# The twist of a coupling network on half-swapped copies made by transfers, and one gelu issued per batch

## The chip, the cores and the metric

The kernel runs on one core of a Trainium2 chip. The metric is the device time of one launch in microseconds (us). The engines are named as the profile names them: PE (TensorE, with PEld for its weight loads), ACT (ScalarE), DVE (VectorE), POOL (GpSimd) and SP (SyncE, which here issues the DMA transfers).

## The reference

The input x has the shape (4, 1024, 128): four batches b, 1024 tokens, 128 channels. Two blocks follow each other. The first is a layer norm, an attention of 16 heads and a gate from a spiking feed-forward net. The second is a layer norm, a causal attention with position slopes, and a gate from the coupling network below; its output is x + attention * silu(network). The change lies in the coupling network alone:

```python
def _coupling_net(h, w1, b1, w2, b2, w3, b3, w4, b4):
    h = _gelu(h @ w1 + b1)          # 128 -> 128
    h = _gelu(h @ w2 + b2)          # 128 -> 64
    h = _gelu(h @ w3 + b3)          # 64 -> 32
    return jax.nn.sigmoid(h @ w4 + b4)
def _twist(x):
    o_r, o_i, p_r, p_i = jnp.split(x, 4, axis=-1)
    return jnp.concatenate([p_r, -p_i, -o_r, o_i], axis=-1)
for _ in range(NUM_CYCLES):         # 3
    tf = _coupling_net(out, ...)
    combined = 0.7 * gf + 0.3 * tf  # gf: one number per batch
    coupling = BASE_COUPLING + adaptive_range * (combined - 0.5) * 2.0
    out = out + coupling * _twist(out)
```

The twist takes channel c from channel c + 64 (or c - 64), with a sign for each quarter of the channels.

## The kernel before

**Stages.** The launch runs through a prologue, `first_attention`, `middle`, and `second_attention`, with a small `row_maxima` between them. `middle` computes the coupling network for all four batches. Each stage ends in a barrier of all engines, so the next one starts when the slowest engine of `middle` is done.

**Layout in `middle`.** The state is transposed: 128 channels on the 128 partitions, 1024 tokens per batch in the free dimension (`state(b)`, a slice of the tile `y`). `half(b, hf)` is a slice of 512 tokens. The four batches form two streams z of two batches k each, so batch = 2z + k. Three cycles of two streams make six rounds n = 0 to 5, with stream z = n % 2 and cycle n // 2. Round n works on the same state as round n - 2.

**One round.** `first_layer(n, k)` multiplies both halves of a batch by w1 (L1592) and gelu follows on ACT as g1b0 or g1b1 (L1404, 128x1024). `second_layer(n, k)` multiplies by w2, its 64 output channels for one token half in partitions 0 to 63 and for the other half in 64 to 127 (L1599). One gelu, `g2`, then covers both batches (L1404, 128x1024). `third_layer(n)` (L1607) writes batch 0 to partitions 0 to 63 and batch 1 to 64 to 127 of one bank, by two column positions of the array; a gelu `g3` follows (L1404, 128x512). `last_layer(n)` (L1620) spreads the single output over all 128 partitions, so the tanh `t0`, `t1` of `couple(n, k)` (L1425, 128x1024) has the same value on each partition. `twist(n, k)` on DVE then updates the state: two operations on 64 partitions each (L1524) compute (t + offset) * state with the source half read crosswise, and a third on 128 partitions (L1527) adds slope times that to the state; slope carries the signs.

**Order.** It is written out by hand on each engine, and each engine keeps its own order. On PE one pass of the loop is `first_layer(n, 0)`, `last_layer(n - 1)`, `first_layer(n, 1)`, `second_layer(n, 0)`, `second_layer(n, 1)`, `third_layer(n)`. On ACT it is `g3` of round n - 1, `g1b0` of n, `t0` and `t1` of n - 1, `g1b1` of n, `g2` of n. On DVE it is `twist(n - 2, 1)`, `twist(n - 1, 0)`. `first_layer(n, k)` waits for `twist(n - 2, k)`. Around this lies side work for the last quarter of the tokens of the next attention: q, k and v rows and norms, with `low`, `high`, `values`, `norm_peak`. It stands in rounds 0, 1 and 5. After the loop DVE has still `low(0, 1)`, `low(1, 1)`, `twist(4, 1)`, `values(1)`, `norm_peak(1)`, `twist(5, 0)`, four small operations on the flag, and `twist(5, 1)`, its last work in the stage.

**Transfers.** SP issues, at the start of `middle`, six loads of `k_st` and `q_st` (L1370, L1372), then two `load_pair` calls of nine transfers each (L224, L227), then the stores of `q_hl` and `k_hl` for hf = 0 and, late, for hf = 1 (L1382). A semaphore `saved` is raised by POOL (L1395) once it has copied the half of the last batch's state that arrives last.

Of the kernel before, what the change touches and what calls it, by code (L numbers as in the profile page):

```python
# [16 lines left out]
F32 = mybir.dt.float32  # L17
# [3 lines left out]
ALU = mybir.AluOpType  # L21
# [3 lines left out]
P = 128  # L25
B, T, C = 4, 1024, 128
# [192 lines left out]
def load_pair(sp, s, layer, b, gp, sem):  # L219

    tok, own, groups = bass.ds(T * b, T), slice(C // 2 * gp, C // 2 * gp + C // 2), slice(2 * gp, 2 * gp + 2)
    for rows, st, order in ((s["q_hl"][layer], s["q_st"], (0, 0, 1)), (s["k_hl"][layer], s["k_st"], (0, 1, 0))):
        for way, hl in enumerate(order):
            sp.dma_start(st[way::WAYS, groups, :].bitcast(F32),  # L224
                         rows[own, hl:hl + 1, tok].rearrange("(g c) o t -> c g (o t)", g=2)).then_inc(sem, 16)
    for e in range(3):
        sp.dma_start(s["q_st"][WAYS * e + EXTRA::STACK, groups, :].bitcast(F32),  # L227
                     s["q_ext"][layer][H * e + H // 2 * gp:H * e + H // 2 * gp + H // 2, tok].rearrange("(g j) t -> j g t", g=2)).then_inc(sem, 16)
# [1049 lines left out]
STREAMS = 2  # L1278
TINY = 1.0e-12
LAYERS = ("w1b0", "w1b1", "w2b0", "w2b1", "w3", "w4")  # L1280
SQUASHES = ("g1b0", "g1b1", "g2", "g3", "t0", "t1")
SIDE_PS = ("mix31", "xt30", "q30", "k30", "xt31", "v30", "n30", "q31", "k31", "v31", "n31")
SIDE_ACT = ("xt30", "q30", "k30", "xt31", "q31", "k31")
SIDE_DVE = ("mix31", "q30", "k30", "v30", "n30", "q31", "k31", "v31", "n31")
# [2 lines left out]
def middle(nc, a, s):  # L1287
# [5 lines left out]
    with ExitStack() as ctx:  # L1293
        def sb(name, shape, dt=F32):
            return ctx.enter_context(nc.sbuf_tensor(f"n_{name}", shape, dt))

        sem = Semaphores(nc, ctx, "n_")

        ROUNDS = STREAMS * CYCLES
        OWN = B - 1  # L1300
        Q = P // 4
        w1, w2, w3, w4, b1, b2, b3, g1, g2, g3, gb1, gb2, scalars = (s["cn"][name] for name in (
            "w1", "w2", "w3", "w4", "b1", "b2", "b3", "g1", "g2", "g3", "gb1", "gb2", "scalars"))
# [8 lines left out]
        gf, offset = sb("gf", [P, B]), sb("offset", [P, B])  # L1312
        h1 = [sb(f"h1_{k}", [C, 2, HALF]) for k in range(2)]
        h2 = sb("h2", [2 * H1, 2, HALF])
        h3 = sb("h3", [4 * H2, HALF])
        th = [[sb(f"th{z}{k}", [P, 2, HALF]) for k in range(2)] for z in range(STREAMS)]
        change = [s["early"][0][:, k, :, :].bitcast(F32) for k in range(2)]
        late = s["early"][1][:, 0, :, :].bitcast(F32)
        mix, xt31 = late[:, 0, :].rearrange("p (t c) -> p t c", c=C), late[:, 1, :]
        square = [s["ext"][0][:, HALF * hf:HALF * hf + HALF].bitcast(BF16).rearrange("p (z t) -> p z t", z=2) for hf in range(2)]  # L1320
# [3 lines left out]
        ps = [ctx.enter_context(nc.psum_tensor(f"n_ps{z}", [P, 4, HALF], F32)) for z in range(STREAMS)]  # L1324
        pa, pb = ps
        layered, squashed, twisted = (sem.many(x, STREAMS) for x in ("layered", "squashed", "twisted"))
# [2 lines left out]
        chain, twist_link, norm1, peaks = sem("chain"), sem("twist_link"), sem("norm1"), sem("peaks")  # L1329
        xs1_rdy, saved, sq_rdy, peak_turned = (sem(x) for x in ("xs1_rdy", "saved", "sq_rdy", "peak_turned"))  # L1330
        ext_in = sem("ext_in")
        stored = [s[f"stored1{hf}"] for hf in range(2)]
        xt = s["y"][:, :, :].rearrange("p t c -> p (t c)")

        def state(b):
            return xt[:, T * b:T * b + T]
# [4 lines left out]
        def tiles(hf):  # L1341
            return slice(BT * OWN + HT * hf, BT * OWN + HT * hf + HT)

        def by_tile(bank):
            return bank.rearrange("p (t c) -> p t c", c=C)

        def layer_count(n, name):
            return len(LAYERS) * (n // 2) + LAYERS.index(name) + 1

        def squash_count(n, name):  # L1350
            return len(SQUASHES) * (n // 2) + SQUASHES.index(name) + 1

        def batch_count(n, k):
            return 2 * (n // 2) + k + 1
# [7 lines left out]
        def dve_count(name):  # L1362
            return SIDE_DVE.index(name) + 1

        with nc.Block() as block:
            @block.sync
            def _(sp):
                for e in range(3, 6):
                    own = slice(WAYS * e + EXTRA, P, STACK)
                    sp.dma_start(s["k_st"][own, :, :].bitcast(F32),  # L1370
                                 s["k_ext"][H * (e - 3):H * (e - 2), :].rearrange("(g j) t -> j g t", g=NG)).then_inc(ext_in, 16)
                    sp.dma_start(s["q_st"][own, :, :].bitcast(F32), s["one_ext"].rearrange("(g j) t -> j g t", g=NG)).then_inc(ext_in, 16)  # L1372
                for hf in range(2):
                    sp.wait_ge(stored[hf], 32 * (B - 1))
                for gp in range(2):
                    load_pair(sp, s, 1, 0, gp, s["staged"][1][gp])
                for hf in range(2):
                    for z in range(2):
                        sp.wait_ge(side_dve, dve_count(f"{'qk'[z]}3{hf}"))
                        rows = (s["q_hl"][1], s["k_hl"][1])[z]  # L1380
                        tok = slice(T * OWN + HALF * hf, T * OWN + HALF * hf + HALF)
                        sp.dma_start(rows[:, :, tok], parts[hf][:, z, :, :].bitcast(F32)).then_inc(stored[hf], 16)  # L1382
                sp.wait_ge(ext_in, 16 * 6)
# [17 lines left out]
            def _(act):  # L1401
                def gelu(n, name, out, source, bias):
                    z = n % 2
                    nc.scalar.activation(out, source, ACT.Gelu, bias=bias[:, 0:1]).then_inc(squashed[z], 1)  # L1404
# [3 lines left out]
                    gelu(n, f"g1b{k}", h1[k][:, :, :], ps[n % 2][:, 2 * k:2 * k + 2, :], b1)  # L1408

                def second_layer(n):  # L1410
                    act.wait_ge(layered[n % 2], layer_count(n, "w2b1"))
                    gelu(n, "g2", h2[:, :, :], ps[n % 2][:, 0:2, :], b2)

                def third_layer(n):
                    act.wait_ge(layered[n % 2], layer_count(n, "w3"))
# [42 lines left out]
                high(0, 0, pb[:, 2, :])  # L1458
                global_layer(0, 1, pb[:, 1, :])
                second_layer(0)  # L1460
                high(1, 0, pb[:, 3, :])
                for n in range(1, ROUNDS):
# [24 lines left out]
            def _(dve):  # L1487
                ch, links, norm = Chain(dve, chain), Chain(dve, twist_link), Chain(dve, norm1)
# [24 lines left out]
                def twist(n, k):  # L1513
                    z = n % 2
                    out, t = state(2 * z + k), th[z][k][:, :, :].rearrange("p h t -> p (h t)")
                    moved = change[k].rearrange("p h t -> p (h t)")
                    if n < 2 and k == 0:
                        dve.wait_ge(offs, z + 1)
                    dve.wait_ge(squashed[z], squash_count(n, f"t{k}"))
                    if n == 1 and k == 1:  # L1520
                        dve.wait_ge(saved, 1)
                    low_half, high_half = slice(0, P // 2), slice(P // 2, P)
                    for dst, src in ((low_half, high_half), (high_half, low_half)):
                        ins = nc.vector.scalar_tensor_tensor(moved[dst, :], t[src, :], offset[src, 2 * z + k:2 * z + k + 1],  # L1524
                                                             out[src, :], ALU.add, ALU.mult)
                    links.after(ins)
                    nc.vector.scalar_tensor_tensor(out, moved, slope[:, 0:1], out, ALU.mult, ALU.add).then_inc(twisted[z], 1)  # L1527

                means(0)
# [18 lines left out]
                ins = nc.vector.tensor_tensor(mix[:, :, :], by_tile(pb[:, 1, :]), s["xn"][:, tiles(1), :], ALU.add)  # L1548
# [14 lines left out]
                ch.wait()  # L1563
                means(1)
                twist(0, 0)
                for n in range(2, ROUNDS):
                    twist(n - 2, 1)
                    twist(n - 1, 0)
# [17 lines left out]
            def _(pe):  # L1586
# [15 lines left out]

                def third_layer(n):
                    z = n % 2
                    pe.wait_ge(squashed[z], squash_count(n, "g2"))
                    for k in range(2):
                        ins = nc.tensor.matmul(ps[z][2 * H2 * k:2 * H2 * k + 2 * H2, 2, :], w3[:, :], h2[:, k, :],  # L1607
                                               start=True, stop=True, tile_position=(0, 2 * H2 * k))
                    ins.then_inc(layered[z], 1)
# [50 lines left out]
                for t in range(HT):  # L1660
                    for gp in range(2):
                        ins = nc.tensor.matmul(pb[:, 1, t * C:(t + 1) * C], on[2 * gp + 1][:, t * P:(t + 1) * P],
                                               s["wo_x"][:, gp, :], start=gp == 0, stop=gp == 1)
# [9 lines left out]
                second_layer(0, 1)  # L1673
                rows_of(1, 0, half(OWN, 0), pb[:, 3, :])
                third_layer(0)
                global_layer(0, 2, pb[:, 1, :])
                turn_in(1)
# [451 lines left out]
```

## Time and profile before

| | us |
|---|---|
| median of 3 runs | 935.69 (935.6 to 936.01) |
| profiled execution, its own time | 938.43 |
| profiled execution, span of the trace | 936.7 |
| `middle` in the trace, first to last instruction | 545.3 to 627.0 |
| PE busy over the span | 809.0 (86%) |
| ACT busy over the span | 834.5 (89%) |
| DVE busy over the span | 409.8 (44%) |

Starts in the trace are counted from the start of the span. A row of the timeline gives the start, the time taken, the engine, the line and the operation, how many instructions were merged into it, and in brackets how long the engine had idled before it and what released it. PEclk is the mean granted clock of TensorE as a share of full speed.

### The profile page before, as it was taken

The numbers are of one execution on the slowest core, as the hardware profiler recorded it, in microseconds if no ns is written. First come the engines' busy times: TensorE is split into PE (matmuls) and PEld (weight loads), VectorE is DVE, ScalarE is ACT, GpSimd is POOL, SyncE is SP. The second block draws the span as 40 slices with busy tenths as digits, with TensorE's granted clock in tenths as the row PEclk, the third lists the DMA queues.
The fourth block names the chain that finished last, engine by engine and source line by source line (L and its number), as shares of the span: only waits on it lengthen the run. The fifth ranks groups of instructions, "written<-read, shape, count | busy, mean of one in ns | idle before, by whom it ended". The sixth has DMA issues, their size and how long they took to land. (4 is left out here: it accounts for less than half of the span.)

```text
span 936.7 us, 23514 instructions
## 1 busy us (share of the span) xinstructions
PE 809.0 (86%) x9998; PEld 328.0 (35%) x9998; DVE 409.8 (44%) x878; ACT 834.5 (89%) x951; POOL 187.9 (20%) x229
## 2 busy tenths in 40 slices
PE   3859999899999999999999988837888878878876
PEld 2412434234343443433334332213333334333323
DVE  7630264443756437473464867770112111121222
ACT  7659999999999999999999945638999999999995
POOL 2201120130202302022120210001214223233133
PEclk9869999999999999999999999978999999999999
DMA  6972020200201202003001151010202202112000
GB/s 177 291 251 41 2 73 2 71 5 2 96 24 43 77 2 96 25 17 103 3 1 47 47 160 46 0 46 1 73 1 85 70 15 84 29 58 85 13 1 24
DMA packets 32049, 53.53 MB, mean 57 GB/s; under 512 B 5576, under 2 KB 16456, under 8 KB 31944
## 3 DMA queue, kind: packets, MB, share of 16 engines
q1 hardware_dynamic: 31944, 52.02, 17.4%
q8 instruction: 80, 1.31, 0.6%
q14 instruction: 25, 0.20, 0.1%
HBM read 31.29 MB, written 20.71 MB: 56 GB/s over the span
## 5 line engine op out<-in xcount | busy, mean ns | idle before, releaser
L983 ACT ACTIVATE a_probs<-a_sc 128x1024 f32<-128x1024 f32 x512 | 474.5, 1031 | 11.3 <-PE a_sc L1182 10.6
L1858 ACT ACTIVATE a_probs<-a_sc 128x1024 f32<-128x1024 f32 (+1 forms) x320 | 273.5, 957 | 31.1 <-PE a_sc L2010 20.2
L1197 PE MATMUL a_o<-a_probs,vt 128*18 128x256 f32 (+1 forms) x3072 | 273.0, 459 | 0.0
L2045 PE MATMUL a_o<-a_probs,vt 128*18 128x256 f32 (+3 forms) x1920 | 153.4, 428 | 0.6 <-POOL a_probs L1884 0.6
L1182 PE MATMUL a_sc<-q_st,k_st 32*128 32x512 f32 x1024 | 131.7, 502 | 23.3 <-ACT a_probs L983 17.7
L2004 PE MATMUL a_sc<-q_st,k_st 32*128 32x512 f32 (+3 forms) x768 | 80.6, 427 | 62.0 <-ACT a_probs L1858 50.5
L1197 PEld LDWEIGHTS a_o<-a_probs,vt 128*18 128x18 f32 x3072 | 65.4, 97 | 144.3 <-issue 104.4
L1884 POOL TENSOR_SCALAR_AFFINE_SELECT a_probs<-a_probs 128x512 f32<-128x512 f32 x96 | 59.7, 646 | 219.3 <-ACT a_probs L1858 219.3
L1182 PEld LDWEIGHTS a_sc<-q_st,k_st 32*128 32x128 f32 x1024 | 50.7, 184 | 138.2 <-ACT a_probs L983 129.1
L2004 PEld LDWEIGHTS a_sc<-q_st,k_st 32*128 32x128 f32 x768 | 37.9, 184 | 127.3 <-ACT a_probs L1858 112.1
L1010 POOL TENSOR_TENSOR early<-early 128x512 f32<-128x512 f32 x32 | 38.4, 1200 | 185.3 <-DVE early L1120 185.3
L1917 DVE STREAM_TRANSPOSE a_turn<-a_o 128x512 f32<-128x512 f32 x15 | 10.8, 717 | 133.1 <-PE a_o L2045 133.1
L2045 PEld LDWEIGHTS a_o<-a_probs,vt 128*18 128x18 f32 x1920 | 41.8, 97 | 69.1 <-issue 45.5
L1120 DVE TENSOR_SCALAR early<-a_side 128x512 f32<-128x512 f32 x32 | 22.0, 687 | 69.0 <-PE a_side L123 69.0
L1124 DVE TENSOR_SCALAR y<-a_side,rho 128x128 f32<-128x128 f32 x32 | 9.0, 344 | 88.2 <-PE a_side L123 88.2
L1404 ACT ACTIVATE n_h<-n_ps,cn_b 128x1024 f32<-128x1024 f32 (+1 forms) x24 | 24.1, 1006 | 22.0 <-PE n_ps L1592 11.8
L996 POOL TENSOR_TENSOR early<-early,y 128x512 f32<-128x512 f32 x7 | 10.6, 1513 | 144.3 <-DVE early L1135 144.3
L1524 DVE SCALAR_TENSOR_TENSOR early<-n_th,n_offset,y 64x1024 f32<-64x1024 f32 x24 | 30.8, 1285 | 10.3 <-ACT n_th L1425 9.9
L123 PE MATMUL a_side<-proj_t,early 128*32 128x128 f32 x1024 | 33.8, 273 | 0.0
L123 PE MATMUL a_side<-y,fc_t 128*32 128x512 f32 x256 | 33.3, 592 | 0.0
L123 PEld LDWEIGHTS a_side<-proj_t,early 128*32 128x32 f32 x1024 | 29.3, 110 | 5.9
L1018 POOL TENSOR_TENSOR a_square<-parts 128x512 bf16<-128x512 f32 x12 | 15.1, 1257 | 80.4 <-DVE parts L1152 80.4
(242 smaller groups left out, 775.9 us busy)
## 6 DMA issues: line engine op xcount, KB each, us to landing
q_st<-q_hl SPq DMA_DIRECT2D x48, 256.0 KB
k_st<-k_hl SPq DMA_DIRECT2D x48, 256.0 KB
q_hl<-parts SPq DMA_DIRECT2D x12, 512.0 KB, 4.3
k_hl<-parts SPq DMA_DIRECT2D x12, 512.0 KB, 4.7
q_hl<-early SPq DMA_DIRECT2D x4, 512.0 KB, 4.8
k_hl<-early SPq DMA_DIRECT2D x4, 512.0 KB, 5.6
out_dram<-x SPq DMA_DIRECT2D x7, 256.0 KB, 3.9
x<-in_L_attn_x_dram SPq DMA_DIRECT2D x3, 512.0 KB, 5.6
```

The costliest lines, as they stand in the source:

```text
L123: ins = nc.tensor.matmul(out[c:c + COLUMN, :], weight[:, c:c + COLUMN], rows, start=start, stop=stop, tile_position=(0, c))
L983: nc.scalar.activation(probs[t % RING][:, 2 * pair:2 * pair + 2, :], scores[unit % SLOTS][:, :, :], ACT.Exp).then_inc(expd, 1)
L1010: pool.tensor_tensor(hidden[f], hidden[f], hidden[f], ALU.mult).then_inc(hid_rdy, 1)
L1120: ins = nc.vector.tensor_scalar_max(hidden[hf[1]], side[:, :], 0.0)
L1182: ins = nc.tensor.matmul(scores[(2 * t + i // 2) % SLOTS][:, i % 2, :], k_st[part, g, kt * P:(kt + 1) * P], q_st[part, g, qh * HALF:(qh + ...
L1197: ins = nc.tensor.matmul(o_ps[32 * h:32 * h + 2 * W9, c0:c1], vt[b % 2][:, kt, gp, h, W9 * gs:W9 * gs + 2 * W9], probs[t % RING][:, h, c0: ...
L1404: nc.scalar.activation(out, source, ACT.Gelu, bias=bias[:, 0:1]).then_inc(squashed[z], 1)
L1524: ins = nc.vector.scalar_tensor_tensor(moved[dst, :], t[src, :], offset[src, 2 * z + k:2 * z + k + 1], out[src, :], ALU.add, ALU.mult)
L1858: nc.scalar.activation(probs[t % RING][:, 2 * pair:2 * pair + 2, 0:width(t)], scores[unit % SLOTS][:, :, 0:width(t)], ACT.Exp).then_inc(ex ...
L1884: ins = pool.affine_select(out=part, in_=part, compare_op=ALU.is_ge, fill=0.0, base=0, pattern=[[0, G], [1, P]], channel_multiplier=-1)
L2004: ins = nc.tensor.matmul(banks[i][:, at:at + w], k_st[part, g, kt * P:(kt + 1) * P], q_st[part, g, qh * HALF + q0:qh * HALF + q0 + w], sta ...
L2045: ins = nc.tensor.matmul(o_ps[32 * h:32 * h + 2 * W9, q0:q0 + w], vt[b % 2][:, kt, gp, h, W9 * gs:W9 * gs + 2 * W9], probs[t % RING][:, h, ...
```

## The change

`twist` reads a copy of the state with its two partition halves swapped, which two transfers per batch and cycle make: `shift(b)` copies rows 64 to 127 of `state(b)` to rows 0 to 63 of `turned[b]`, and the reverse. With it the two crosswise operations become one on 128 partitions, in place on the copy. The copies of batches 0 to 2 are issued first of all in `middle`, that of batch 3 after `saved`, and those of the later cycles by `shift_again(n)`, after `twist(n, k)`. The gelu of the second layer is issued once per batch (`g2b0`, `g2b1`, each 128x512), and `third_layer` waits for each.

```diff
-SQUASHES = ("g1b0", "g1b1", "g2", "g3", "t0", "t1")
+SQUASHES = ("g1b0", "g1b1", "g2b0", "g2b1", "g3", "t0", "t1")
...
-        change = [s["early"][0][:, k, :, :].bitcast(F32) for k in range(2)]
+        turned = [s["early"][0][:, k, :, :].bitcast(F32).rearrange("p h t -> p (h t)") for k in range(2)]
+        turned += [s["early"][1][:, 1, :, :].bitcast(F32).rearrange("p h t -> p (h t)"), s["ext"][1][:, :]]
...
+        shifted = sem.many("shifted", B)
...
             @block.sync
             def _(sp):
+                def shift(b):
+                    for rows, source in ((slice(0, P // 2), slice(P // 2, P)), (slice(P // 2, P), slice(0, P // 2))):
+                        sp.dma_start(turned[b][rows, :], state(b)[source, :]).then_inc(shifted[b], 16)
+
+                def shift_again(n):
+                    for k in range(2):
+                        sp.wait_ge(twisted[n % 2], batch_count(n, k))
+                        shift(2 * (n % 2) + k)
+
+                for b in range(OWN):
+                    shift(b)
...
+                sp.wait_ge(saved, 1)
+                shift(OWN)
                 for hf in range(2):
+                    if hf == 1:
+                        for n in range(ROUNDS - STREAMS):
+                            shift_again(n)
...
                 def second_layer(n):
-                    act.wait_ge(layered[n % 2], layer_count(n, "w2b1"))
-                    gelu(n, "g2", h2[:, :, :], ps[n % 2][:, 0:2, :], b2)
+                    for k in range(2):
+                        act.wait_ge(layered[n % 2], layer_count(n, f"w2b{k}"))
+                        gelu(n, f"g2b{k}", h2[:, k, :], ps[n % 2][:, k, :], b2)
...
-                    moved = change[k].rearrange("p h t -> p (h t)")
+                    moved = turned[2 * z + k]
...
-                    low_half, high_half = slice(0, P // 2), slice(P // 2, P)
-                    for dst, src in ((low_half, high_half), (high_half, low_half)):
-                        ins = nc.vector.scalar_tensor_tensor(moved[dst, :], t[src, :], offset[src, 2 * z + k:2 * z + k + 1],
-                                                             out[src, :], ALU.add, ALU.mult)
-                    links.after(ins)
+                    dve.wait_ge(shifted[2 * z + k], 32 * (n // 2 + 1))
+                    links.after(nc.vector.scalar_tensor_tensor(moved, t, offset[:, 2 * z + k:2 * z + k + 1], moved, ALU.add, ALU.mult))
                     nc.vector.scalar_tensor_tensor(out, moved, slope[:, 0:1], out, ALU.mult, ALU.add).then_inc(twisted[z], 1)
...
                 def third_layer(n):
                     z = n % 2
-                    pe.wait_ge(squashed[z], squash_count(n, "g2"))
                     for k in range(2):
+                        pe.wait_ge(squashed[z], squash_count(n, f"g2b{k}"))
                         ins = nc.tensor.matmul(ps[z][2 * H2 * k:2 * H2 * k + 2 * H2, 2, :], w3[:, :], h2[:, k, :],
                                                start=True, stop=True, tile_position=(0, 2 * H2 * k))
                     ins.then_inc(layered[z], 1)
```

## Rows read from the trace of the kernel before

**Rows 1.** Groups by line and shape, 540 to 640 us: busy us, mean ns, idle before.

```profile
L1524 DVE SCALAR_TENSOR_TENSOR early<-n_th,n_offset,y 64x1024 f32<-64x1024 f32 x24 | 30.8, 1285 | 10.3 <-ACT n_th L1425 9.9
...
L1404 ACT ACTIVATE n_h<-n_ps,cn_b 128x1024 f32<-128x1024 f32 x18 | 20.0, 1114 | 17.3 <-PE n_ps L1592 11.8 <-PE n_ps L1599 5.5
L1527 DVE SCALAR_TENSOR_TENSOR y<-early,n_slope,y 128x1024 f32<-128x1024 f32 x12 | 15.4, 1284 | 0.4
...
L1404 ACT ACTIVATE n_h<-n_ps,cn_b 128x512 f32<-128x512 f32 x6 | 4.1, 683 | 4.7 <-PE n_ps L1607 4.7
```

**Rows 2.** Timeline of one pass of the loop, up to the gelu of round 4.

```profile
591.82 1.08 PE L1607 MATMUL n_ps<-n_h,cn_w 128*64 128x512 f32 x4 [1.21 <-ACT n_h L1404]
592.83 1.98 PE L1592 MATMUL n_ps<-y,cn_w 128*128 128x512 f32 x4
...
594.04 1.28 DVE L1527 SCALAR_TENSOR_TENSOR y<-early,n_slope,y 128x1024 f32<-128x1024 f32 x1
...
594.85 1.11 ACT L1404 ACTIVATE n_h<-n_ps,cn_b 128x1024 f32<-128x1024 f32 x1 [1.22 <-PE n_ps L1592]
...
595.81 1.98 PE L1592 MATMUL n_ps<-y,cn_w 128*128 128x512 f32 x4
595.95 2.12 ACT L1425 ACTIVATE n_th<-n_ps,n_half_b 128x1024 f32<-128x1024 f32 x2
...
597.96 1.11 ACT L1404 ACTIVATE n_h<-n_ps,cn_b 128x1024 f32<-128x1024 f32 x1
...
599.13 1.08 PE L1599 MATMUL n_ps<-n_h,cn_w 128*64 128x512 f32 x4 [0.32 <-ACT n_h L1404]
...
600.25 1.11 ACT L1404 ACTIVATE n_h<-n_ps,cn_b 128x1024 f32<-128x1024 f32 x1 [1.18 <-PE n_ps L1599]
```

**Rows 3.** Timeline of two narrow windows within `third_layer(4)`.

```profile
601.42 0.65 PE L1607 MATMUL n_ps<-n_h,cn_w 128*64 128x512 f32 x2 [1.22 <-ACT n_h L1404]
...
601.90 0.60 PE L1607 MATMUL n_ps<-n_h,cn_w 128*64 128x512 f32 x2
```

**Rows 4.** Timeline of the end of `middle` and the first matmul after it.

```profile
612.29 0.75 DVE L1492 SCALAR_TENSOR_TENSOR parts<-n_ps,b_col,parts 128x512 fp32r<-128x512 f32 x1 [1.03 <-ACT parts L1436]
...
613.07 2.67 DVE L1524 SCALAR_TENSOR_TENSOR early<-n_th,n_offset,y 64x1024 f32<-64x1024 f32 x2
...
614.99 2.12 ACT L1425 ACTIVATE n_th<-n_ps,n_half_b 128x1024 f32<-128x1024 f32 x2 [1.49 <-PE n_ps L1620]
...
618.48 2.58 DVE L1524 SCALAR_TENSOR_TENSOR early<-n_th,n_offset,y 64x1024 f32<-64x1024 f32 x2
...
623.09 2.58 DVE L1524 SCALAR_TENSOR_TENSOR early<-n_th,n_offset,y 64x1024 f32<-64x1024 f32 x2
625.70 1.28 DVE L1527 SCALAR_TENSOR_TENSOR y<-early,n_slope,y 128x1024 f32<-128x1024 f32 x1
...
629.88 0.80 PE L2004 MATMUL a_sc<-q_st,k_st 32*128 32x512 f32 x4 [11.12 <-DVE a_o L1961]
```

**Rows 5.** Waits by engine and line, 545 to 627 us: us in total, times, longest.

```profile
ACT n_h L1404 <- PE n_ps L1599: 5.5, 6, 1.2
```

**Rows 6.** Timeline of SP, POOL, PE and DVE at the start of `middle`.

```profile
545.28 0.57 SPq L1370 DMA_DIRECT2D k_st<-k_ext  x1
...
560.10 0.61 SPq L1382 DMA_DIRECT2D q_hl<-parts  x1
560.26 0.61 POOL L1395 COPY early<-y 128x512 f32<-128x512 f32 x1 [1.12 <-ACT y L1430]
...
571.93 3.68 PE L1592 MATMUL n_ps<-y,cn_w 128*128 128x512 f32 x4
...
581.90 2.58 DVE L1524 SCALAR_TENSOR_TENSOR early<-n_th,n_offset,y 64x1024 f32<-64x1024 f32 x2
```

**Rows 7.** Windows: busy us of PE, PEld, DVE, ACT, POOL; PEclk, DMA share, GB/s.

```profile
557.00:561.00 4.00, 3.84 (x21) 1.66 (x21) 3.12 (x8) 2.61 (x6) 1.90 (x3) 1.00 0.92 300
...
573.00:577.00 4.00, 4.00 (x13) 1.12 (x12) 0.36 (x1) 1.36 (x2) 0.00 (x0) 0.69 0.02 4
```

**Rows 8.** DMA issues of the whole span: count, size, us to landing.

```profile
q_hl<-parts SPq DMA_DIRECT2D x12, 512.0 KB, 4.3
...
k_hl<-early SPq DMA_DIRECT2D x4, 512.0 KB, 5.6
```

## Prediction

> **What bounds the kernel now.** Three views were read, in this order. The groups by line and shape give each operation's price: a twist is two operations of 1.285 us on 64 partitions and one of 1.284 us on 128, and a gelu costs 1.114 us for 1024 columns and 0.683 us for 512 [rows 1]. Next the timeline of one pass of the loop, to see who waits for whom. The third layer starts at 591.82 and again at 601.42, so a pass takes 9.60 us [rows 2, 3]. Between them runs one chain, each link starting where the one before ends: third layer (start to next start 1.01 us), first layer of batch 0 (2.02), g1b0 (1.10), the two tanh (2.01), g1b1 (1.11), then 0.06 to the second layer of batch 1 (1.12 with the handover), g2 (1.11) and 0.06 to the next third layer [rows 2]. They add up to 9.60. ACT idles 1.18 us ahead of g2, waiting for the second layer of batch 1, while the result of batch 0 has been ready. DVE isn't in this chain: its twist of batch 1 ends at 594.04 + 1.28 = 595.32, and the first layer that needs it starts at 595.81, behind the last layer on PE, so DVE has 0.49 us to spare [rows 2]. Last the end of the stage. DVE works from 612.29 on with three twists, at 613.07, 618.48 and 623.09, and ends at 626.98, while ACT's last tanh ends at 617.11 [rows 4]. The next stage's first matmul stands at 629.88, 2.90 us behind DVE's end [rows 4]. So in the loop the ACT and PE chain decides, and after it DVE alone.
>
> **Twist: the loop.** 12 times two operations of 1.285 become one. The trace has no such operation in place on 128 partitions, but L1527 is the same instruction of the same shape, also with its output over its second input, at 1.284 us [rows 1]; I take that. A twist falls from 3.9 to 2.6 us. In the loop this is worth nothing by itself, since DVE isn't in the chain. It is what lets the pass get shorter: without it, a pass shorter by more than 0.49 us would run into DVE.
>
> **Twist: the end.** Three twists stand between 612.29 + 0.75 and the end. The first begins when `low(1, 1)` is done. The second needs t0 of round 5, which is done at 614.99 + 1.06 = 616.05; without the first twist's saving its place is 618.48, with it 618.48 - 1.30 = 617.18, so no wait opens there [rows 4]. The third needs t1 (617.11) and stands behind the flag operations, at 623.09 - 2.60 = 620.49. Each saves 2.58 - 1.28 = 1.30 us: 3 x 1.30 = **3.9 us**. The additional wait on `shifted` in front of each is met long before; the smallest handover in [rows 2] that contains a wait is 0.06 us, so it costs 0 to 3 x 0.06 = 0.2 us; I take 0, since such a wait can be passed while the operation ahead still runs.
>
> **The gelu per batch.** With an idle time w ahead of g2, the old order ends at w + 1.114. In the new one g2b0 starts at once and g2b1 at the later of w and 0.683, and ends 0.683 later. For w = 1.18 that is 2.294 against 1.863: 0.43 us. All six waits total 5.5 [rows 5]; rounds 1 to 4 with the 1.18 of [rows 2] make 4.7, which leaves 0.8 for rounds 0 and 5, where side work stands in the gap. With w = 0.4 each, the end goes from 1.51 to 1.37, 0.15 us. In round 5 what follows on the way to DVE is `high(1, 1)`, which also needs a side matmul that PE runs at that time, so I count 0.15 for round 0 and 0 for round 5.
> Then the third layer. It is tempting to count half of it too, since batch 0's half can now run ahead. But two of its matmuls start together at 601.42 and two at 601.90 [rows 3]: the halves, on different columns of the array, already run side by side, and the half of batch 1 alone takes as long as both. So nothing is gained there: 4 x 0.43 + 0.15 = **1.9 us**.
> The split itself costs 2 x 0.683 - 1.114 = 0.25 us of ACT a round [rows 1]. It lies in the 1.18 us idle before g2b1; uncovered it would cost 6 x 0.25 = 1.5 us and the gain of 1.9 would be gone with it.
> The Trainium skill ("VectorE: DVE Perf Modes", on the TRN2 errata) says that each instruction pays a fixed cost, which it puts at 172 cycles at 1.2 GHz for ScalarE reading PSUM, so small tiles lose. By its formula a pair of halves takes 1.14 us against 1.00, 0.14 a round instead of 0.25. The rows agree with the direction and have the larger number.
>
> **The transfers.** 12 copies of 2 x 256 KB. An issue takes 0.57 us on SP [rows 6], so the first six delay all that follows by some 3.4 us: the `load_pair` data, for the next stage at 629.88, and the q and k stores of hf = 0, which went out at 560.10 and now at some 564.7. The fourth copy goes ahead of them, at about 560.10 + 3.4 = 563.5; `saved` was raised at 560.87 [rows 6], so SP doesn't wait for it. DMA is busy at 0.92 and moves 300 GB/s there [rows 7]. The extra 1.5 MB take 5 us at that rate. A 512 KB transfer lands 4.3 to 5.6 us after its issue [rows 8]; with a backlog of 5 us on top the fourth copy lands at 574 at the latest. Its reader, `twist(1, 1)`, stood at 581.90 [rows 6] and would stand near 581.90 - 1.30 - 0.6 = 580.0. It is covered by 6 us. Later copies have two passes less a twist, 2 x 9.17 - 2.6 = 15.7 us, for 5.6 us. SP reaches the late stores of hf = 1 after `twist(3, 1)`, well ahead of the side work in round 5. So 0.
> By the Trainium skill ("SBUF — State Buffer", on the DMA port swizzle) a transfer over 64 partitions reaches only half the ports, 196 GB/s at 1 MiB, and two such transfers don't add up. The 1.5 MB would take 8 us instead of 5 and the cover shrink to about 3 us; no time changes.
>
> **Sum.** 3.9 + 1.9 = 5.8 us. The profiled execution would go from 938.43 to 932.6 of its own time (span 936.7 to 930.9). The median of the runs lies 2.74 below that execution, and nothing in the change touches what makes that difference, so 935.69 - 5.8 = **929.9 us**.
>
> **Rivals.**
> *The clock comes back (928.2 us).* The first layer of round 2 took 3.68 us where the same takes 1.98 [rows 6, 2]; the granted clock was 0.69 over 573 to 577, so part of it ran at 1.2 GHz [rows 7]. PE had been waiting ahead of the third layer just before. That hole now holds the half of batch 0, so the clock may not fall: 3.68 - 1.98 = 1.7 us more. Against it: a fall may come at another place instead, and the runs shown may not have had it.
> *The halves of the third layer take turns (927.7).* Then half of 1.08 us is saved per round as well, 4 x 0.54 = 2.2 more. [Rows 3] speak against it.
> *The split gives nothing (931.8).* If waits between the two gelus and two matmul groups eat 0.43 us, only 3.9 remain. Handovers of 0.06 [rows 2] speak against it.
> *The copies come late, and it is slower.* The place is `twist(1, 1)` on DVE. The first layer behind it stood one pass ahead of 595.81, at 586.21 [rows 2], so the twist may start as late as 586.2 - 0.6 - 2.6 = 583.0, and each us later lengthens the chain. To eat 5.8 us the fourth copy must land at 588.8, 25 us after its issue; at 590.7 it is 0.2% slower, 937.6. The rows have 5.6 us for a landing [rows 8]. The same would hold if each later copy took over 15.7 us.
>
> **How the numbers follow.** Forecast 929.9 (within 1 us): 0.50. Clock: 0.22. Turns: 0.06. Split gives nothing: 0.12. Late copies: 0.04. None of these: 0.06. The next stage begins at the low clock in any case, and when that ends relative to its first matmuls may move the time by up to 1 us either way. The range 927.3 to 932.1 holds the forecast, the clock and the case without the split, and leaves out most of the rest. About 0.2% (1.9 us) is what a measurement of this kernel can tell from no change: faster 0.92, within 0.04, slower 0.04, the last being the late copies.
>
> **What would show it.** L1524's successor: 12 operations of 128x1024 at 1.28 us with no wait for a DMA. A pass of 9.17 us between two third layers. ACT's idle ahead of the second-layer gelus split into a short one before g2b1 (about 0.5). The second half of `third_layer` taking as long as both did. The last three twists at 2.6 us each, DVE's end at 621.2, and the next stage's first matmul 2.9 us behind. Wrong would be: DVE waiting for DMA, DVE in the chain of the loop, or a stage end set by another engine than DVE.

## The result, and the profile after

| | before | after |
|---|---|---|
| median, 10 runs each | 935.9 us (934.72 to 938.72) | 929.25 us (928.43 to 933.92) |
| ratio after / before | | 0.9928 (95%: 0.9912 to 0.9945) |
| profiled span | 936.7 | 927.2 |
| entry of `middle` (first L1592, now L1608) | 545.33 | 542.68 |
| end of `middle` (last twist) | 626.98 | 616.98 |
| entry to end | 81.65 | 74.30 |
| from there to the end of the span | 309.75 | 310.26 |

929.25 us against 929.9 forecast; the medians differ by 6.65 us where 5.8 was summed, and the interval of the ratio reaches from 5.1 to 8.2 us. The two profiled spans differ by 9.5 us, and this may not be read as the change: 2.65 of it lie ahead of `middle`, where nothing was edited. The rest is taken apart below. The 2.65 us go with TensorE's clock early in the launch, which the windows from 20 to 80 us of the two traces show (PEclk behind the five engines, 0.74 in the kernel before, 0.86 in the kernel after):

```profile
20.00:80.00 60.00, 41.20 (x210) 17.21 (x214) 27.20 (x89) 37.34 (x53) 6.29 (x8) 0.74 0.70 223
```

```profile
20.00:80.00 60.00, 39.46 (x242) 16.66 (x242) 27.62 (x93) 40.20 (x56) 6.28 (x8) 0.86 0.69 224
```

Of the thirteen traces of this document eight have 0.74 there and an entry of `middle` at 543.98 to 545.43, the other five have 0.80 to 0.86 and an entry at 542.49 to 543.44.

**Groups by line and shape**, of the kernel after, 540 to 640 us; they answer to [rows 1].

```profile
L1422 ACT ACTIVATE n_h<-n_ps,cn_b 128x1024 f32<-128x1024 f32 x12 | 13.4, 1114 | 10.1 <-PE n_ps L1608 10.1
...
L1422 ACT ACTIVATE n_h<-n_ps,cn_b 128x512 f32<-128x512 f32 x18 | 12.1, 685 | 6.5 <-PE n_ps L1623 4.2 <-PE n_ps L1615 2.4
L1542 DVE SCALAR_TENSOR_TENSOR early<-n_th,n_offset,early 128x1024 f32<-128x1024 f32 x9 | 11.8, 1307 | 17.4 <-ACT n_th L1444 17.3
L1543 DVE SCALAR_TENSOR_TENSOR y<-early,n_slope,y 128x1024 f32<-128x1024 f32 x9 | 11.6, 1285 | 0.3
...
L1542 DVE SCALAR_TENSOR_TENSOR ext<-n_th,n_offset,ext 128x1024 f32<-128x1024 f32 x3 | 3.8, 1280 | 0.0
```

Twelve operations on 128 partitions (9 and 3, by the buffer of the copy) stand for 24 on 64, at nearly the same price each. DVE's idle time ahead of them grew from 9.9 to 17.3 us and is put down to ACT but for 0.1: no DMA is among the releasers, so no copy was waited for.

**One pass of the loop**, timeline of the kernel after; it answers to [rows 2].

```profile
583.18 1.69 ACT L1422 ACTIVATE n_h<-n_ps,cn_b 128x1024 f32<-128x1024 f32 x2
...
584.35 1.08 PE L1615 MATMUL n_ps<-n_h,cn_w 128*64 128x512 f32 x4 [0.32 <-ACT n_h L1422]
...
585.26 2.03 PE L1623 MATMUL n_ps<-n_h,cn_w 128*64 128x512 f32 x4
...
585.48 0.69 ACT L1422 ACTIVATE n_h<-n_ps,cn_b 128x512 f32<-128x512 f32 x1 [0.60 <-PE n_ps L1615]
...
586.22 0.19 PEld L1623 LDWEIGHTS n_ps<-n_h,cn_w 128*64 128x64 f32 x2 [0.82 <-ACT n_h L1422]
587.22 0.30 PEld L1608 LDWEIGHTS n_ps<-y,cn_w 128*128 128x128 f32 x2 [0.81 <-issue]
```

The first row holds two instructions, g1b1 (1.11 us) and, straight behind it, g2b0: the name of the group is that of the first. ACT's idle time ahead of the second-layer gelus is now 0.60 us instead of 1.18, and g2b1 takes 0.69 instead of 1.11. Of the third layer batch 0's half now starts at 585.26 and batch 1's at 586.22, and from there to the next group on PE it is 1.00 us, as it was for both halves together [rows 3, 2].

**The end of the stage**, timeline of the kernel after; it answers to [rows 4].

```profile
606.25 0.75 DVE L1511 SCALAR_TENSOR_TENSOR parts<-n_ps,b_col,parts 128x512 fp32r<-128x512 f32 x1 [1.31 <-ACT parts L1455]
...
606.91 1.50 DVE L1542 SCALAR_TENSOR_TENSOR early<-n_th,n_offset,early 128x1024 f32<-128x1024 f32 x1
...
611.14 1.28 DVE L1542 SCALAR_TENSOR_TENSOR early<-n_th,n_offset,early 128x1024 f32<-128x1024 f32 x1
...
614.37 1.28 DVE L1542 SCALAR_TENSOR_TENSOR ext<-n_th,n_offset,ext 128x1024 f32<-128x1024 f32 x1
615.69 1.28 DVE L1543 SCALAR_TENSOR_TENSOR y<-ext,n_slope,y 128x1024 f32<-128x1024 f32 x1
...
619.88 0.80 PE L2020 MATMUL a_sc<-q_st,k_st 32*128 32x512 f32 x4 [8.45 <-DVE a_o L1977]
```

DVE still ends the stage, and the next one's first matmul is 2.91 us behind it, as before (2.90). The 1.50 us of the first twist's first operation is taken up in the last section.

**The transfers**, timeline of SP and DVE, and the DMA issues from 530 to 625 us, of the kernel after.

```profile
542.63 4.84 SPq L1372 DMA_DIRECT2D early<-y  x6
...
562.52 1.18 SPq L1372 DMA_DIRECT2D ext<-y  x2
...
575.73 1.28 DVE L1542 SCALAR_TENSOR_TENSOR ext<-n_th,n_offset,ext 128x1024 f32<-128x1024 f32 x1
```

```profile
early<-y SPq DMA_DIRECT2D x18, 256.0 KB, 4.7
...
ext<-y SPq DMA_DIRECT2D x6, 256.0 KB, 4.4
```

The fourth copy leaves at 562.5 to 563.7 and takes 4.4 us, so it is there near 568, and its reader starts at 575.73: some 8 us of cover.

**The stage in parts.** The starts of the first layer's matmuls on PE mark its rounds. This table holds, for every trace, the time from the entry to the first layer of round 1, then to that of round 2, then the mean of the three passes from round 2 to round 5, and from round 5 to the end of the stage; all in us, from the starts in the timelines. It carries the verdicts below, since the parts behind round 1 repeat within 0.05 us in traces of the same kernel, but for the one pass of 11.29 us in the first trace of before, while the medians of the kernel after were 929.25 and 932.24 us (e7).

| kernel | entry to round 1 | round 1 to 2 | pass, rounds 2 to 5 | round 5 to end | entry to end |
|---|---|---|---|---|---|
| before, first trace | 14.99 | 11.61 | 10.17 (11.29, 9.61, 9.60) | 24.56 | 81.65 |
| before, again (e10) | 16.52 | 11.61 | 9.60 | 24.56 | 81.50 |
| before, again (e11) | 15.26 | 11.61 | 9.60 | 24.56 | 80.23 |
| after | 15.02 | 11.18 | 9.17 | 20.59 | 74.30 |
| after, again (e7) | 16.37 | 11.18 | 9.17 | 20.59 | 75.65 |
| gelu alone (e1) | 15.95 | 11.17 | 9.17 | 24.56 | 79.19 |
| twist alone (e2) | 16.55 | 11.61 | 9.60 | 20.60 | 77.57 |
| no transfers (e3) | 14.74 | 11.17 | 9.17 | 20.56 | 73.98 |
| fourth copy late (e5) | 16.28 | 11.18 | 9.87 (9.16, 11.28, 9.17) | 20.59 | 77.66 |
| half of the third layer, in before (e6) | 16.52 | 11.60 | 9.59 | 24.55 | 81.46 |
| early twist (e4) | 14.78 | 11.17 | 9.17 | 19.39 | 72.84 |
| early twist, again (e8) | 15.04 | 11.18 | 9.17 | 19.38 | 73.10 |
| early twist, POOL held back (e9) | 15.96 | 11.18 | 9.17 | 19.37 | 74.03 |

The first column depends on how long TensorE stays at 1.2 GHz behind the entry: until 2.8 to 2.9 us behind it in the first trace of before, e3 and e4, until 3.7 in e11 and 3.9 in the kernel after, and until 6.0 us in e10 and 6.2 in e7. Two pairs of before and after agree in this, and they are the ones to compare: 80.23 - 74.30 = 5.93 us and 81.50 - 75.65 = 5.85 us.

### The profile page after: what moved, and what is told of

It is laid out like the page before. It is cut to its first block and busy times, and to the rows that moved or that the text cites. A ratio compares the mean times of both kernels' runs of the same rounds, so it can differ in the third digit from the quotient of the medians.

```text
span 927.2 us, 23540 instructions
## 1 busy us (share of the span) xinstructions
PE 807.7 (87%) x9998; PEld 327.9 (35%) x9998; DVE 394.5 (43%) x866; ACT 835.2 (90%) x957; POOL 187.4 (20%) x229
## 5 line engine op out<-in xcount | busy, mean ns | idle before, releaser
L1422 ACT ACTIVATE n_h<-n_ps,cn_b 128x512 f32<-128x512 f32 (+1 forms) x30 | 25.0, 857 | 16.6 <-PE n_ps L1608 10.1
L123 PE MATMUL a_side<-wo_x,on 128*32 128x128 f32 x896 | 29.7, 273 | 0.0
```

What stands on the lines that cost most here:

```text
L123: ins = nc.tensor.matmul(out[c:c + COLUMN, :], weight[:, c:c + COLUMN], rows, start=start, stop=stop, tile_position=(0, c))
```

## Experiments

Each ran on the chip beside the kernel before; ratios are to it, with 95% intervals.

**e1, the gelu per batch alone.** The kernel before, with only this part of the change.

```diff
-SQUASHES = ("g1b0", "g1b1", "g2", "g3", "t0", "t1")
+SQUASHES = ("g1b0", "g1b1", "g2b0", "g2b1", "g3", "t0", "t1")
...
-                    act.wait_ge(layered[n % 2], layer_count(n, "w2b1"))
-                    gelu(n, "g2", h2[:, :, :], ps[n % 2][:, 0:2, :], b2)
+                    for k in range(2):
+                        act.wait_ge(layered[n % 2], layer_count(n, f"w2b{k}"))
+                        gelu(n, f"g2b{k}", h2[:, k, :], ps[n % 2][:, k, :], b2)
...
-                    pe.wait_ge(squashed[z], squash_count(n, "g2"))
                     for k in range(2):
+                        pe.wait_ge(squashed[z], squash_count(n, f"g2b{k}"))
```

> Only the gelu per batch, with the twist in three operations as before. My theory: rounds 1 to 4 lose 0.43 us each and round 0 another 0.15, so 1.9 us off 935.7 (ratio 0.998), a pass of 9.17 us, DVE's cover ahead of the first layer of batch 1 down from 0.49 to 0.06 us, and the end of the stage still 14 us of DVE. Rival (the halves of the third layer take turns): 4 us off. Rival (the split needs the shorter twist): the pass stays above 9.3 us and the gain under 1.5 us. Rival (the clock): the fall of TensorE's clock in round 2 is gone here too, and 1.7 us more comes off, 3.6 us in all.

Measured: 933.15 us, ratio 0.9969 (0.9955 to 0.9983), that is 1.6 to 4.2 us off. In the table the passes are 0.43 and 0.44 us shorter, four of them, and the end is untouched. How near DVE comes to the chain, its timeline shows:

```profile
590.54 1.28 DVE L1528 SCALAR_TENSOR_TENSOR y<-early,n_slope,y 128x1024 f32<-128x1024 f32 x1
591.89 0.30 PEld L1593 LDWEIGHTS n_ps<-y,cn_w 128*128 128x128 f32 x2 [0.76 <-DVE y L1528]
```

The twist ends at 591.82, 0.07 us ahead of the matmul that needs it. So the split needs no shorter twist, but only just, and the rival that it does is out.

**e2, the twist alone.** The kernel after, with the lines above turned back.

> Only the twist on swapped copies, with one gelu for both batches as before. My theory: the loop keeps its pass of 9.60 us, and the three last twists give 3 x 1.30 = 3.9 us (ratio 0.996). Rival (the end is not DVE's alone): less than 3 us. Rival (the clock hole is what matters): the fall in round 2 stays, since the hole ahead of the third layer stays, so nothing beyond 3.9 us.

Measured: 931.97 us, ratio 0.995 (0.9933 to 0.9968). The passes stay at 9.60 to 9.61, the part behind round 5 falls from 24.56 to 20.60, by 3.96 us. The expectation's rival let the fall of the clock in round 2 stay as long as PE's idle time ahead of the third layer (the hole) stays. The hole is there, the fall isn't.

**e3, no transfers.**

```diff
-                        sp.dma_start(turned[b][rows, :], state(b)[source, :]).then_inc(shifted[b], 16)
+                        pass
...
-                    dve.wait_ge(shifted[2 * z + k], 32 * (n // 2 + 1))
-                    links.after(nc.vector.scalar_tensor_tensor(moved, t, offset[:, 2 * z + k:2 * z + k + 1], moved, ALU.add, ALU.mult))
+                    links.after(nc.vector.scalar_tensor_tensor(moved, t, offset[:, 2 * z + k:2 * z + k + 1], out, ALU.add, ALU.mult))
```

> The changed kernel without any of the 24 transfers; the twist reads the state itself instead of a swapped copy, so the crosswise part of the computation is left out. My theory (transfers fully hidden): the same time as the changed kernel within 0.5 us, some 929.3. Rival (the transfers slow the engines or are waited for): 1 us or more faster than the changed kernel; the first operation of twist(4, 1), 1.50 us in the changed kernel against 1.28 elsewhere, then tells whether it was a transfer that stretched it.

Measured: 930.71 us, ratio 0.9933 (0.9916 to 0.9949), against 0.9928 for the kernel after. The time is 1.5 us above the 929.3 expected, outside the 0.5, but in another series of runs, and e7 has the kernel after itself at 932.24. The stage settles it: from round 1 on the parts are the same within 0.03 us, and the entry takes 14.74 us against 14.78 in e4, which has the transfers and the same length of slow clock. The 24 transfers cost nothing that shows. The stretched operation is stretched here too:

```profile
609.24 1.50 DVE L1541 SCALAR_TENSOR_TENSOR early<-n_th,n_offset,y 128x1024 f32<-128x1024 f32 x1
...
608.62 1.04 POOL L1409 TENSOR_TENSOR ext<-parts 128x512 bf16<-128x512 f32 x1 [1.02 <-ACT parts L1455]
```

**e4 and e8, the twist of round 4 ahead of the late rows.**

```diff
+                twist(ROUNDS - 2, 1)
                 low(0, 1, pa[:, 0, :])
                 low(1, 1, pa[:, 1, :])
-                twist(ROUNDS - 2, 1)
```

> The changed kernel with twist(4, 1) put ahead of low(0, 1) and low(1, 1) on DVE, into the 0.9 and 1.3 us for which DVE idles there. My theory (DVE alone sets the end, from the last tanh t0 on): twist(5, 0) moves up until it waits for t0 at 609.8 instead of starting at 611.14, so 1.3 us off the changed kernel, 928.0. Rival (the late rows, which low now gives later, hold up the end, by the norm peak): no gain or a loss of some 0.5 us.

> twist(4, 1) ahead of low(0, 1) and low(1, 1), beside the changed kernel on the same chip. From the entry of round 5 to the end of the stage 19.4 us against 20.6, so 1.2 us less of the whole, 0.1%; the runs alone may not tell it apart.

Measured: e4 929.57 us, where 928.0 was expected, ratio 0.9926 (0.991 to 0.9942); e8 929.64 us, ratio 0.9924 (0.9909 to 0.9938), with the kernel after on the same chip (e7) at 932.24 us, 0.9939 (0.9919 to 0.9958). The intervals overlap, so the runs don't tell it from the kernel after. The traces do, for the stage: 19.38 and 19.39 us against 20.59 behind round 5, 1.2 us less in both, where the first expectation had 1.3. Of the kernels tried this is the one with the shortest stage. In its timeline the move met POOL:

```profile
606.45 1.13 POOL L1409 TENSOR_TENSOR ext<-parts 128x512 bf16<-128x512 f32 x1 [43.63 <-ACT parts L1455]
...
606.72 1.94 DVE L1543 SCALAR_TENSOR_TENSOR y<-early,n_slope,y 128x1024 f32<-128x1024 f32 x1
```

**e5, the fourth copy late.**

```diff
                 sp.wait_ge(saved, 1)
+                sp.wait_ge(twisted[1], 1)
                 shift(OWN)
```

> The changed kernel, with SP waiting for the end of twist(1, 0) before it issues the copy of the fourth batch. The copy then leaves at about the end of twist(1, 0) (577.0 plus the offset of the stage in its own trace would be 575.8 in the changed kernel's) and lands 4.5 us later; twist(1, 1) waits on DVE for it instead of starting at once. My theory (the cover is the distance to the first layer of round 3, batch 1): twist(1, 1) would start 4.7 us late, has about 2.2 us of room, and the stage gets 2 to 3 us longer than the changed kernel's 74.3, 76.5 us. Rival (the loop has more room than I think): under 1 us. Rival (the late copy also pushes the copies behind it on SP, round after round): more than 4 us.

Measured: 933.76 us, ratio 0.9963 (0.9949 to 0.9978). The timeline shows issue, wait and damage:

```profile
578.95 1.18 SPq L1372 DMA_DIRECT2D ext<-y  x2
...
583.66 1.28 DVE L1543 SCALAR_TENSOR_TENSOR ext<-n_th,n_offset,ext 128x1024 f32<-128x1024 f32 x1 [4.80 <-DMA ext<-y]
584.98 1.28 DVE L1544 SCALAR_TENSOR_TENSOR y<-ext,n_slope,y 128x1024 f32<-128x1024 f32 x1
586.32 1.99 PE L1609 MATMUL n_ps<-y,cn_w 128*128 128x512 f32 x4 [2.17 <-DVE y L1544]
588.43 1.28 DVE L1543 SCALAR_TENSOR_TENSOR early<-n_th,n_offset,early 128x1024 f32<-128x1024 f32 x1 [2.16 <-DMA early<-y]
```

The copy is there 4.7 us behind its issue. DVE is 4.80 us late, PE 2.17, and the pass from round 3 to 4 takes 11.28 us instead of 9.17, 2.11 more; the next pass is 9.17 again, though DVE waits once more for a copy that SP issued late behind this one. So the room was 4.8 - 2.1 = 2.7 us at this place, where the prediction had 3.0 and the expectation 2.2. That beyond the room each us costs one is how I read it; one delay was tried. The stage's 77.66 us hold 1.26 us of slower clock at the entry (16.28 us to round 1 against 15.02).

**e6, half of the third layer.** In the kernel before:

```diff
                     pe.wait_ge(squashed[z], squash_count(n, "g2"))
-                    for k in range(2):
+                    for k in (1,):
```

> The kernel before, with the third layer's matmuls for the first batch of each stream left out in all rounds; that part of the computation is missing. My theory (the two halves run side by side on different columns): the pass between two third layers stays at 9.60 us and the next group on PE starts 1.01 us after it. Rival (the halves take turns): the next group starts 0.5 us after it and the pass shrinks to about 9.1 us.

Measured, in a single run: 936.9 us, with the kernel before at 936.21 in the same series. Its timeline:

```profile
590.29 1.07 PE L1607 MATMUL n_ps<-n_h,cn_w 128*64 128x512 f32 x2 [1.22 <-ACT n_h L1404]
591.29 1.99 PE L1592 MATMUL n_ps<-y,cn_w 128*128 128x512 f32 x4
...
599.88 1.07 PE L1607 MATMUL n_ps<-n_h,cn_w 128*64 128x512 f32 x2 [1.21 <-ACT n_h L1404]
```

Two matmuls instead of four take 1.07 us instead of 1.08, the next group starts 1.00 us on, and the pass is 9.59. The halves run side by side.

**e7, the kernel after once more.**

> The changed kernel unaltered, beside the next one on the same chip. Within 0.3% of 929.3. By my reading of the first traces the fall of the clock in round 2 hangs on how PE's idle times meet the chip's own timing, so no fall between the entry and the end of the stage here again if the filled hole is what matters, or one some of the time if it is chance.

Measured: 932.24 us (928.98 to 934.31), 0.32% above 929.25 and so just outside the 0.3%; no fall of the clock in the loop. Behind round 1 the stage has the same parts.

**e9, POOL held back.** In the kernel of e4:

```diff
                     spread(pool, s, b)
+                pool.wait_ge(twisted[0], batch_count(ROUNDS - 2, 1))
                 squares(1)
```

> The kernel with the early twist(4, 1), and POOL's squares of the second half held back until that twist is done. In the kernel without this wait the twist's second operation took 1.94 us instead of 1.28 while POOL multiplied two operands from SBUF (1.13 us) beside it. My theory (the two take turns at something when both read two operands from SBUF): the operation is back at 1.28 us, with the stage's end unchanged within 0.2 us, since values(1) behind it waits for PE. Rival (the position in the code or the ACT writes at that time stretch it): it stays above 1.5 us.

Measured, in a single run: 928.55 us. From round 5 to the end it is 19.37 us, as in e4. The twist is back at its price:

```profile
605.85 1.29 DVE L1544 SCALAR_TENSOR_TENSOR y<-early,n_slope,y 128x1024 f32<-128x1024 f32 x1
...
607.22 2.04 POOL L1409 TENSOR_TENSOR ext<-parts 128x512 bf16<-128x512 f32 x2 [45.26 <-DVE y L1544]
```

**e10 and e11, the kernel before twice more.**

> The kernel before, unaltered, for another trace. If the fall of the clock in round 2 comes from PE's idle time ahead of the third layer, it is there again, and the first layer of round 2 takes 3.7 us. If it is chance how the idle times meet the chip's own timing, it may be missing, and the pass from round 2 to round 3 takes 9.6 us instead of 11.3.

> As the one before, a third trace of the kernel before: with the fall 81.7 us from the entry of the stage to its end, without it some 80.0.

Measured, in one run each: 937.79 and 936.9 us, with the kernel before at 937.07 in the same series. Neither trace has a fall of the clock in round 2. Windows over the first layer and what follows, of the first trace of before and of e11 (PEclk behind the five engines):

```profile
571.90:575.60 3.70, 3.70 (x9) 1.15 (x9) 1.42 (x2) 0.78 (x3) 0.00 (x0) 0.54 0.02 4
```

```profile
569.30:573.00 3.70, 3.70 (x16) 1.45 (x16) 1.45 (x2) 2.43 (x5) 0.00 (x0) 1.00 0.02 4
```

The same code, in the same place of the stage: 9 matmuls in 3.7 us at a granted clock of 0.54, 16 at 1.00. What PE did before is the same too: in both traces it idled 1.16 us ahead of the third layer of round 1 and 0.34 us ahead of the small matmuls behind it.

## Why the prediction was right

**The end of the stage: right.** 3.9 us were summed for three twists. From round 5 to the end it was 24.56 us in all three traces of before and 20.59 after, 3.97 less, and e2 gets 3.96 alone. That the sum fits so well is in part luck. From a twist's start to that of what follows it (or to its own end, for the last) the second and the third save 1.29 us each, but the first only 1.17, since its first operation is stretched by POOL in the kernel after (1.50 us; the pair had 2.67 before). The missing 0.15 is made good by 0.21 that wasn't forecast: the first twist now starts 0.66 us behind the start of the operation ahead of it instead of 0.78, and the third 0.08 instead of 0.17 ([rows 4] and the end of the stage above; 614.29 and 622.92 are the starts of the last flag operation).

**The gelu: right, with its reason.** 4 x 0.43 us: the pass from round 1 to 2 is 0.43 shorter and the next three 0.43 each. The decisive step was to read that the third layer's halves start together [rows 3], and so to count only ACT's part; e6 confirms that half of the layer takes as long. Counting half of the third layer as well would have given 8 us. Round 0 gives 0.24 us between e11 and after, 0.15 between e10 and e7 and 0.21 between the first trace of before and e4, pairs with slow clocks of nearly the same length, where 0.15 was forecast; and round 5 gives nothing, as forecast: 20.59 with the split and 20.60 without.

**The two parts add up.** e1 has the loop of the kernel after with the end of before, e2 the reverse. The shorter twist wasn't needed for the shorter pass: DVE had 0.49 us to spare, the split takes 0.43, and 0.07 remain.

**The transfers: right in the result, with a term off.** An issue was priced at 0.57 us, and the first six took 4.84, 0.81 each; the fourth copy left 19.8 us behind the entry instead of 18.2. It had 8 us of cover rather than 6: the backlog of 5 us that I allowed for didn't delay its landing, 4.4 us, and nothing of the 3 us of cover that a halved rate would leave shows. Against that the reader came 1.6 us earlier than forecast (33.1 us behind the entry instead of 34.7), since the forecast counted from a trace with the fall of the clock ahead of it. The rival of the late copies has nearly the price that it was given: e5 shows 2.11 us for a delay of 4.8, where a room of 3.0 would have left 1.8.

**The sum: 5.8 forecast, 5.9 measured in the stage**, between traces with the same clock at the entry. The medians say 6.65, with an interval of 5.1 to 8.2 that holds it. What makes up the difference isn't the edit as far as the traces show: the entry of `middle` lies at 542.5 in one trace of before (e11) and at 544.9 and 545.3 in the others, with the same code ahead of it, and goes with the clock early in the launch (0.86 against 0.74 and 0.74). Behind the stage the same code takes 309.7 us in e10 and 312.5 in e11. The prediction allowed up to 1 us either way for that; the two differ by 2.8. Neither was in the sum, and that the medians came so near to it is luck to that extent.

**The rival of the clock.** The first trace of after had no fall in round 2 where that of before had one, 1.7 us. It was tempting to credit the filled hole. Of five traces with the hole (three of before, e2, e6) only that one has a fall; of the eight with the hole filled, none has. So the 11.29 us pass of the first trace is no fixed part of the kernel before. Whether the filled hole makes such a fall rarer, one in five against none in eight can't tell; that stays open. It was right to leave it out of the sum.

## What to carry to other kernels

Find the chain that closes on itself in one pass of a loop, add its links up until they give the period, and count from an edit only what it takes out of that chain; then look at the stage's end by itself, where another engine may be alone. Before counting half of a group of matmuls, look whether the halves start together. And compare two traces stage by stage, from marks inside them: a difference between two whole spans also holds what the clock did differently from launch to launch, here 3.6 of 9.5 us.

## What the runs showed of the hardware

**A DVE operation with two inputs in SBUF is stretched beside a POOL one that reads SBUF.** The same twist operation took 1.28 us alone, 1.50 where it overlapped a POOL multiplication by 0.42 us (e3, and the kernel after), 1.94 where it overlapped by 0.86 us (e4), and 1.29 when POOL was made to wait (e9). The Trainium skill ("SBUF — State Buffer", on who interferes with whom) says that a VectorE instruction with two SBUF inputs contends with a GpSimd one that reads SBUF, and the traces agree. The excess, 0.22 and 0.66 us, is the overlap less 0.20 in both cases. DVE's operation on `parts`, which takes its other input from PSUM, isn't stretched: 0.75 us at 606.25 in the kernel after, with POOL's from 606.29 on beside it. Nor is it always DVE that pays. In the kernel before the twist's operation had begun first:

```profile
609.31 1.28 DVE L1527 SCALAR_TENSOR_TENSOR y<-early,n_slope,y 128x1024 f32<-128x1024 f32 x1
...
610.27 1.22 POOL L1391 TENSOR_TENSOR ext<-parts 128x512 bf16<-128x512 f32 x1 [47.04 <-ACT parts L1436]
```

There DVE keeps its 1.28 us and POOL takes 1.22 instead of 1.04, in all three traces of before and in e6, and 1.23 in e1; in e4 POOL's 1.13 us begin 0.23 us before the end of the twist's first operation. So it is the operation that begins second that is stretched in every case here. The copies stretched nothing: the parts of the stage are the same without them (e3).

**A transfer over 64 partitions from SBUF to SBUF isn't slow here.** Two of 256 KB each are there 4.4 to 4.7 us behind the issue, where 512 KB in one transfer over 128 partitions to DRAM took 4.3 to 5.6 [rows 8]. At what rate many such transfers would go, no run measures. An issue costs SP 0.55 to 0.81 us where it waits for nothing, so a pair costs twice that in its queue.
